# Adaptive attention and expert kernel on one core: the first three slots of a software pipeline written out one by one

## The chip, the cores and the metric

The kernel runs on one core of a Trainium2 chip. The metric is the device time of one execution in microseconds (us), the median of the runs shown. The engines of the core are TensorE (PE in the profile, with PEld for its weight loads), VectorE (DVE), ScalarE (ACT), GpSimd (POOL) and SyncE (SP). SP and ACT also issue DMA transfers from queues of their own (SPq, ACTq), and POOL issues the gathers.

## The reference

The input x has 64 samples of 64 rows and 1024 columns. With one adapter (A, B) out of 64 and one 64x64 mixing matrix for each sample:

```python
z  = (x @ B[i].T) @ A[i].T                     # rank 16
f  = rfft(z); corr = irfft(f * conj(f))        # autocorrelation of each row, length 1024
w, delay = top_k(corr, 6); w = softmax(w)
x  = x + sum_k w[k] * roll(z, -delay[k])
u  = einsum('bct,bcd->bdt', x, W[cond])        # a 64x64 matrix for each sample
p  = top_k(softmax(u @ W_router.T), 2), normalised
x  = x + u @ W_base.T + b_base + 2 * sum_e p[e] * (u @ A_stack[e].T) @ B_stack[e].T
```

All is float32 to the outside.

## The kernel before

A tile is two samples, 128 rows of x, so there are 32 tiles. Adapters are prepared in groups of eight samples, one group for four tiles. For a group the kernel loads A (eight transfers of 64 KB), sets the samples side by side (`a_beside`, ACT), transposes (`a_transposed`, PE, then `a_out`, ACT), folds it about its symmetry axes (`folds`, POOL), transposes the folds (`fold_transposed`, `fold_out`) and multiplies them by cosines and sines (`a_spectrum`, 18 matmuls). Both A and its spectrum are split in a high and a low part (`g_hi`, `g_lo`), since products of float32 accuracy are made of three matmuls (`three`). For each tile three rectangles of `g_hi` and `g_lo` are copied by DMA into one stack of 96 partitions, `adapter` (`load_adapter`), so that one matmul for 128 columns does the three products at once.

The main loop has slots s = 0 to 34. Slot s does the attention part of tile s, and, `LAG` = 3 slots later, the feed-forward part of tile t = s - 3. The steps of tile s in a slot are: transposes of x (`x_transposed`, `x_out`), x times B (`b_times_x`, `bx_masked`, `bx_repeated`), `stack_high` and `stack_low`, `spectrum` (8 matmuls), its square (ACT), `powers` (POOL, six instructions), `adapter_out` for the values y, which go to DRAM, `eo_hi` and `eo_lo`, and `correlation` (14 matmuls of 256 columns). In the next slot DVE finds the six largest (`top_delays`, L876 to L896), POOL gathers five rolled rows of y from DRAM (`gather`, L1085), and DVE adds them with their weights (`add_y` L909, `add_rolled` L917). `mixed` (PE) then multiplies by the mixing matrices, and the feed-forward part is `project` (L556), `router`, `base` (96 matmuls of 512 columns) and `experts`.

Each engine executes its own list of instructions in the order written, and waits on semaphores. `correlation(s)` is the last thing of a slot on PE; `project(t)` the first of the next. Ahead of the slots, each engine has a prologue written by hand. The eight blocks of W_base are loaded, transposed (`w_transposed`), and split (`w_high` on ACT, `w_low` on DVE): blocks 0 to 5 before slot 0, blocks 6 and 7 in slot 0. The lists of SP and PE begin so:

```python
            load_a(0)
            load_row(0)
            sp.wait_ge(bst_side, 1)
            load_b(0, row[2])
            ...
            load_mix(0)
            load_adapter(0, 0, 0)
            for m in range(KC - 2, KC):
                load_w(sp, m)
            load_a(1)
            slots(slot)
```

ACT first issues the loads of the expert and router weights, which PE transposes before all else, L645 and L646. In slots 0 to 2 there is no feed-forward part.

## Time and profile before

| | |
|---|---|
| median of 3 runs | 867.39 us (866.89 to 869.89) |
| the profiled execution | 867.77 us, with a span of 865.8 us from first to last instruction |
| PE busy | 782.6 us, 90% of the span |
| DVE, POOL, ACT busy | 655.7, 531.1, 328.9 us |
| TensorE clock granted, mean | 0.965 of full speed |
| first `project` (start of slot 3) | 108.90 us |
| ends of the first two correlations | 62.1 and 83.9 us |

All positions are microseconds from the start of the span. "Busy" leaves out waits. An engine's list of idle times names what ended each wait.

### The profile page before, as it was taken

What the parts mean: (1) busy time and instruction counts of PE and PEld (TensorE: products, weight loads), DVE (VectorE), ACT (ScalarE), POOL (GpSimd) and SP (SyncE); (2) the same over time, 40 slices, a digit from 0 to 9 for tenths busy, and PEclk for the clock granted to TensorE, in tenths of its full rate; (3) what the DMA queues carried; (4) which work ended last, traced back from release to release, by engine and by line L of the source; (5) the groups of instructions that cost most, each with busy time, mean ns of one, the idle gap of its engine ahead of it and who ended that gap; (6) DMA issues with size and microseconds to landing.
All of it is one profiled execution on the core that took longest, in us unless ns stands there. A gap on an engine that the chain in (4) does not pass through costs nothing.

```text
span 865.8 us, 14359 instructions
## 1 busy us (share of the span) xinstructions
PE 782.6 (90%) x4808; PEld 650.5 (75%) x4808; DVE 655.7 (76%) x1362; ACT 328.9 (38%) x616; POOL 531.1 (61%) x464
## 2 busy tenths in 40 slices
PE   5655699899998999899998999899998999999897
PEld 4544588778877888778786888778886888878686
DVE  1335588987888787987878888888878888888852
ACT  4453334334443434334443335334443333333211
POOL 0326576846686666856486676856696676666621
PEclk9756699999999999999999999999999999999999
DMA  8477678776877688776877698786878687786621
GB/s 269 139 226 222 193 252 256 243 242 196 268 239 243 211 259 256 241 238 196 252 243 238 210 279 240 225 231 219 259 242 240 216 251 246 240 242 197 192 76 48
DMA packets 65804, 194.26 MB, mean 224 GB/s; under 512 B 13596, under 2 KB 23228, under 8 KB 62532
## 3 DMA queue, kind: packets, MB, share of 16 engines
q0 software_dynamic: 23040, 83.90, 32.4%
q1 hardware_dynamic: 30932, 70.80, 28.4%
q10 hardware_dynamic: 11760, 38.66, 11.6%
q8 instruction: 38, 0.62, 0.3%
q14 instruction: 34, 0.28, 0.1%
HBM read 117.82 MB, written 50.33 MB: 194 GB/s over the span
## 4 chain that ended last, share of the span: by engine, by line
PE 51%; POOL 18%; DVE 13%; issue 6%; ACT 5%; DMA 4%; SPq 1%; ACTq 1%; POOLq 0%; DVEq 0%
PE o_ps L437 25%; POOL turn L1108 5%; PE h_ps L556 5%; PE x_ps L461 4%; PE c_ps L437 4%; POOL rolled L1085 4%; PE x_ps L545 3%; POOL row L1071 3%; DVE row L917 3%; POOL eo L1111 3%; POOL eo L1112 3%; DMA y_d<-y 2%; PE t_ps L514 2%; PE t_ps L491 2%; ACT eo_hi L791 2%
## 5 line engine op out<-in xcount | busy, mean ns | idle before, releaser
L1085 POOL DMA_INDIRECT rolled<-y_d,off x160 | 209.1, 1307 | 202.5 <-DVE mirror L885 97.5
L917 DVE SCALAR_TENSOR_TENSOR row<-rolled,weight,row 128x1024 f32<-128x1024 f32 x160 | 221.2, 1383 | 12.5 <-DMA rolled<-y_d,off 6.6
L437 PE MATMUL o_ps<-wt_hi,x_hi 128*128 128x512 f32 x512 | 219.9, 429 | 0.0
L437 PE MATMUL o_ps<-wt_hi,x_lo 128*128 128x512 f32 x512 | 203.3, 397 | 0.0
L437 PE MATMUL o_ps<-wt_lo,x_hi 128*128 128x512 f32 x512 | 203.0, 396 | 0.0
L437 PEld LDWEIGHTS o_ps<-wt_hi,x_hi 128*128 128x128 f32 x512 | 97.5, 190 | 22.0 <-issue 4.6
L437 PEld LDWEIGHTS o_ps<-wt_hi,x_lo 128*128 128x128 f32 x512 | 96.4, 188 | 23.3
L437 PEld LDWEIGHTS o_ps<-wt_lo,x_hi 128*128 128x128 f32 x512 | 97.1, 190 | 15.5
L1071 POOL TENSOR_TENSOR row<-row,bias 128x1024 f32<-128x1024 f32 x32 | 78.0, 2437 | 17.8 <-PE x_ps L545 17.2
L731 ACT ACTIVATE turn<-t_ps 128x512 f32<-128x512 f32 x64 | 34.9, 596 | 132.4 <-PE t_ps L491 132.4
L1108 POOL TENSOR_TENSOR turn<-turn 128x256 f32<-128x256 f32 x64 | 74.3, 1180 | 2.6
L545 PEld LDWEIGHTS x_ps<-mix,row 128*128 128x128 f32 x512 | 61.6, 192 | 16.5 <-ACT r L677 12.0
L545 PE MATMUL x_ps<-mix,row 128*128 128x128 f32 x512 | 63.0, 276 | 11.0 <-ACT r L677 9.4
L556 PE MATMUL h_ps<-aw,turn 128*128 128x136 f32 x512 | 64.6, 279 | 0.0
L556 PEld LDWEIGHTS h_ps<-aw,turn 128*128 128x128 f32 x512 | 61.7, 190 | 0.1
L858 DVE TENSOR_TENSOR eo_lo<-eo,eo_hi 128x640 fp32r<-128x640 f32 x32 | 26.4, 824 | 43.8 <-ACT eo_hi L791 43.7
L942 DVE TENSOR_SCALAR rp<-rex,rinv 128x2 f32<-128x2 f32 x32 | 58.1, 1817 | 1.1
L763 ACT ACTIVATE turn<-t_ps 128x1024 f32<-128x1024 f32 x32 | 32.8, 1025 | 62.6 <-PE t_ps L514 62.6
L858 DVE TENSOR_TENSOR x_lo<-x_ps,x_hi 128x512 fp32r<-128x512 f32 x64 | 42.6, 687 | 17.5 <-ACT x_hi L804 17.5
L437 PE MATMUL c_ps<-back_hi,eo_hi 128*128 128x256 f32 x128 | 39.4, 308 | 16.0 <-DVE eo_lo L858 16.0
L1104 POOL TENSOR_TENSOR eo<-turn 1x128 f32<-1x128 f32 x32 | 14.9, 466 | 60.6 <-ACT turn L763 60.6
L802 ACT ACTIVATE turn<-x_ps 128x512 f32<-128x512 f32 x64 | 38.1, 596 | 27.9 <-PE x_ps L545 27.9
(129 smaller groups left out, 1464.8 us busy)
## 6 DMA issues: line engine op xcount, KB each, us to landing
y_d<-y ACTq DMA_DIRECT2D x64, 512.0 KB
row<-in_x SPq DMA_DIRECT2D x32, 512.0 KB, 7.4
adapter<-g_hi SPq DMA_DIRECT2D x64, 256.0 KB, 5.4
out<-row SPq DMA_DIRECT2D x32, 512.0 KB, 6.0
adapter<-g_lo SPq DMA_DIRECT2D x32, 256.0 KB, 5.7
r<-in_L_cond_A SPq DMA_DIRECT2D x64, 64.0 KB, 4.0
r<-in_L_cond_B SPq DMA_DIRECT2D x56, 64.0 KB
rolled<-in_L_ffn_W_base SPq DMA_DIRECT2D x5, 512.0 KB, 6.1
```

Source lines behind the costliest of these rows:

```text
L437: last = pe.matmul(dst, a, b, start=start and n == 0, stop=stop and n == len(todo) - 1)
L461: return pe.matmul(dst, ft[0:rows, c, :], dft_m[0:rows, at0:at0 + width], start=start, stop=stop, skip_group_check=True)
L545: last = pe.matmul(x_ps[:, c * P:(c + 1) * P], row[t % NROW][:, c * P:(c + 1) * P], mix[t % NMIX][:, :], start=True, stop=True)
L556: last = pe.matmul(h_ps[:, 0:HW], x2[:, c, :], aw[:, c, :], start=c == 0, stop=c == KC - 1)
L731: act.activation(xt[:, 4 * h:4 * h + 4, :].rearrange("p k c -> p (k c)"), t_ps[:, h * 512:(h + 1) * 512], ACT.Copy).then_inc(xt_out, 1)
L802: act.activation(x2[:, 4 * h:4 * h + 4, :].rearrange("p k r -> p (k r)"), x_ps[:, h * 512:(h + 1) * 512], ACT.Copy).then_inc(x2_f, 1)
L858: return dve.tensor_tensor(dst, src, hi.bitcast(F32), ALU.subtract)
L917: dve.scalar_tensor_tensor(rows[:, :], from_buffer[:, :], weight[:, n:n + 1], rows[:, :], ALU.mult, ALU.add).then_inc(sum_step, 1)
L942: step(dve.tensor_scalar(rp[:, :], rex[:, :], rinv[:, :], LORA_SCALE, ALU.mult, ALU.mult))
L1071: pool.tensor_tensor(rows[:, :], rows[:, :], bias[:, :], ALU.add).then_inc(biased, 1)
L1085: pool.indirect_dma_start(out=rolled[at % RB][:, :], out_offset=None, in_=y2_d[u], in_offset=bass.IndirectOffsetOnAxis(ap=off[s % 2][:, n: ...
L1108: step(pool.tensor_tensor(pw[a], pw[a], sq[:, a, 1, :, :].rearrange("p h r -> p (h r)"), ALU.add), a == 1)
```

## The change

Slots 0 to 2 are taken out of the loop, which now begins at `FILL` = 3. Their steps are written out on each engine in a new order, together with the preparation of the weights.

```diff
+            half = GS // 2
+            first = []
+            for s in range(half):
+                first.append(sample_id(s, NS - 1))
+                sample_a(s, first[s])
             load_row(0)
+            for s in range(GS):
+                sample_b(s, first[s] if s < half else sample_id(s, NS - 1), row[4])
+            load_w(sp, 0)
+            (b_stack, a_stack, w_router: 3 loads)
+            second = [sample_id(GS + s, NS - 1) for s in range(GS)]
+            sp.wait_ge(g_h, 1); sp.wait_ge(g_lo_at, 1); sp.wait_ge(f1, 3)
+            for s in range(GS):
+                sample_a(s, second[s])
+            load_w(sp, 1) ... load_w(sp, 3); load_adapter(1, 1, 0); load_row(1); load_w(sp, 4)
+            load_mix(0); load_mix(1); load_adapter(2, 2, 0); load_row(2)
+            load_w(sp, 5); load_w(sp, 6); load_mix(2); load_adapter(3, 3, 0); load_w(sp, 7)
+            load_b(1); load_row(3); (bias); load_mix(3)
+            slots(slot, FILL)
```

ACT issues the load of the identity, then samples 4 to 7 of A, then the cosine tables. `folds(0)` and `folds(1)` run on DVE, as does the low part of A of group 0; later groups stay on POOL. Tile 0 uses `g_hi` and `g_lo` where they are, with three matmuls for each product:

```diff
+            def spectrum0():
+                for c in range(KC):
+                    cols = slice(c * P, (c + 1) * P)
+                    last = three(t_ps[:, cols], [((g_hi[0:TR, 1, cols], g_lo[0:TR, 1, cols]),
+                                                  (s_t[0:TR, :], s_low0))], True, True)
+            def adapter_out0():
+                for h in range(2):
+                    last = three(t_ps[:, cols], [((s_t[0:TR, :], s_low0),
+                                                  (g_hi[0:TR, 0, cols], g_lo[0:TR, 0, cols]))], True, True)
```

PE's list becomes:

```diff
+            a_transposed(0); x_transposed(0); b_transposed(0, row[4], o_ps); fold_transposed(0)
+            b_times_x(0, 0, 0); w_transposed(0); a_spectrum(0, False); bx_repeated(0)
+            a_spectrum(0, True); aw_transposed(); spectrum0(); w_transposed(1); adapter_out0()
+            w_transposed(2); a_transposed(1); x_transposed(1); b_times_x(1, 1, 0); bx_repeated(1)
+            correlation(0)
+            w_transposed(3); spectrum(1, 1, 0); adapter_out(1, 1); fold_transposed(1)
+            w_transposed(4); bs_transposed(); x_transposed(2); b_times_x(2, 2, 0); bx_repeated(2)
+            correlation(1)
+            w_transposed(5); spectrum(2, 2, 0); a_spectrum(1, False); adapter_out(2, 2)
+            a_spectrum(1, True); w_transposed(6); w_transposed(7); mixed(0)
+            correlation(2)
+            slots(slot, FILL)
```

A block of W is now transposed, and split, in two halves of four chunks, always through `o_ps`, and each block has a buffer of its own. On ACT, slot work of tile 1 is ordered exp(0), fold_out(1), w_high(4), y_copy(1), y_store(1), eo_high(1), x_out(2). On DVE the order around the correlations is: folds(1), top_delays(0), weights(0), add_y(0), w_low(3), add_rolled(0,0), w_low(4), eo_low(1), bx_masked(2), add_rolled(0,1), stack_low(2), top_delays(1), bs_low, add_rolled(0,2), w_low(5), add_rolled(0,3), add_rolled(0,4), spectrum_low(1), w_low(6), weights(1), add_y(1), w_low(7), add_rolled(1,0), eo_low(2), mixed_low(0), add_rolled(1,1), add_rolled(1,2). On POOL: powers(0), gather(0, first three), powers(1), gather(0, last two), gather(1, first three), powers(2), gather(1, last two), a_low(1), wait for the bias. The loop body from slot 3 on is unchanged.

## Rows read from the trace of the kernel before

**Rows 1.** The page: busy time of the engines
```profile
PE 782.6 (90%) x4808; PEld 650.5 (75%) x4808; DVE 655.7 (76%) x1362; ACT 328.9 (38%) x616; POOL 531.1 (61%) x464
```

**Rows 2.** Windows: before the first three correlations end, and the rest; last columns clock, DMA share, GB/s
```profile
0.00:62.05 62.05, 35.77 (x190) 29.84 (x191) 15.54 (x14) 29.41 (x34) 13.05 (x23) 0.78 0.70 212
62.05:83.91 21.86, 10.70 (x60) 8.74 (x59) 12.86 (x25) 6.60 (x11) 15.62 (x19) 0.63 0.73 217
83.91:108.90 24.99, 17.63 (x86) 13.46 (x85) 15.19 (x30) 9.59 (x16) 12.68 (x12) 0.71 0.68 205
108.90:865.80 756.90, 718.46 (x4480) 598.44 (x4478) 612.08 (x1293) 283.34 (x555) 489.77 (x411) 1.00 0.73 226
```

**Rows 3.** Timeline of the preparation of group 0
```profile
3.76 8.18 SPq L350 DMA_DIRECT2D r<-in_L_cond_A  x8
...
12.37 1.97 PE L443 MATMUL o_ps<-const,r 128*128 128x128 f32 x8
...
17.30 1.09 PE L443 MATMUL x_ps<-const,r 128*128 128x128 f32 x8 [1.26 <-ACT r L677]
...
18.43 2.08 ACT L677 ACTIVATE r<-x_ps 128x512 f32<-128x512 f32 x2
...
20.59 1.26 POOL L1047 TENSOR_TENSOR r<-r 128x511 f32<-128x511 f32 x1 [19.21 <-ACT r L677]
...
26.82 0.19 POOL L1061 COPY r<-r 128x2 f32<-128x2 f32 x1
```

**Rows 4.** Timeline from the spectrum of group 0 to tile 0's first product
```profile
31.32 4.45 PE L461 MATMUL x_ps<-dft_m,r 128*128 128x258 f32 x18
...
45.58 1.94 PE L514 MATMUL t_ps<-s_t,adapter 96*128 96x128 f32 x8 [2.38 <-DMA adapter<-g_hi]
```

**Rows 5.** Chain of waits, last transfer of group 1's A
```profile
53.57 3.17 DMA r<-in_L_cond_A
```

**Rows 6.** Costliest groups of DVE and ACT up to 110 us, busy us and mean ns
```profile
L917 DVE SCALAR_TENSOR_TENSOR row<-rolled,weight,row 128x1024 f32<-128x1024 f32 x8 | 10.6, 1328 | 5.1 <-DMA rolled<-y_d,off 4.7
L858 DVE TENSOR_TENSOR wt_lo<-o_ps,wt_hi 128x1024 fp32r<-128x1024 f32 x5 | 6.1, 1223 | 10.2 <-ACT wt_hi L677 10.2
L858 DVE TENSOR_TENSOR bs_lo<-o_ps,bs_hi 128x1024 fp32r<-128x1024 f32 x1 | 2.0, 2034 | 16.4 <-ACT bs_hi L677 16.4
L858 DVE TENSOR_TENSOR x_lo<-x_ps,x_hi 128x512 fp32r<-128x512 f32 x2 | 1.4, 692 | 0.3 <-ACT x_hi L804 0.3
L956 DVE TENSOR_TENSOR eo<-t_ps,const 128x128 f32<-128x128 f32 x3 | 0.8, 283 | 0.0
L786 ACT ACTIVATE t_ps<-y 128x1024 f32<-128x1024 f32 x3 | 3.1, 1028 | 2.7 <-ACT y L775 2.7
```

**Rows 7.** Windows of PE alone: busy, clock granted, DMA share
```profile
26.00:30.00 4.00, 2.93 (x14) 0.50 0.88 330
30.00:34.00 4.00, 4.00 (x23) 0.96 0.02 5
92.00:98.00 6.00, 6.00 (x18) 0.50 0.92 309
```

**Rows 8.** Timeline of slots 2 and 3 on PE and DVE
```profile
91.17 5.09 PE L461 MATMUL x_ps<-dft_m,r 128*128 128x258 f32 x10
...
97.65 3.72 PE L461 MATMUL x_ps<-dft_m,r 128*128 128x256 f32 x8
...
116.64 0.29 DVE L956 TENSOR_TENSOR eo<-t_ps,const 128x128 f32<-128x128 f32 x1 [0.50 <-PE t_ps L501]
```

**Rows 9.** Chain of waits: two correlations, base products, a stacked spectrum
```profile
80.59 2.90 PE c_ps L437 x12
107.15 1.67 PE c_ps L437 x12
113.19 2.80 PE o_ps L437 x12
...
119.78 0.84 PE t_ps L514 x8
```

More of the change, by code:

```diff
@@ L669, in _ @@
[L669 to L671 removed]
+            pe.wait_ge(w_l, 2)
+            aw_transposed()
+            spectrum0()
+            pe.wait_ge(st_out, 3)
+            w_transposed(1)
+            adapter_out0()
+            w_transposed(2)
+            a_transposed(1)
+            x_transposed(1, 0)
+            x_transposed(1, 1)
+            b_times_x(1, 1, 0)
+            bx_repeated(1)
+            pe.wait_ge(back_l, 1)
+            correlation(0)
@@ new lines, in _ @@
+            act.wait_ge(cleared, 1)
+            act.dma_start(mid_st, v["back"][:, 4 * Q:5 * Q]).then_inc(back_in, 16)
+            a_out(0)
+            a_high(0, 3, -1)
+            x_out(0, -LAG)
+            b_out(0, o_ps)
+            fold_out(0)
+            w_high(0)
+            stack_high(0)
+            act.wait_ge(back_in, 32)
+            copy(back_hi[:, 0:4, :].rearrange("p a c -> p (a c)"), back_st[:, :]).then_inc(back_h, 1)
+            copy(back_hi[:, 4, :], mid_st).then_inc(back_h, 1)
@@ L838, in _ @@
+            y_copy(0)
+            y_store(0, 0)
+            a_beside(1)
             w_high(2)
-            a_high(0, 3, -1)
-            act.wait_ge(back_in, 32)
-            copy(back_hi[:, 0:4, :].rearrange("p a c -> p (a c)"), y[:, :]).then_inc(back_h, 1)
-            copy(back_hi[:, 4, :], turn[:, 0:Q]).then_inc(back_h, 1)
-            fold_out(0)
-            b_out(0, o_ps)
+            eo_high(0)
+            x_out(1, -LAG)
+            a_out(1)
+            stack_high(1)
+            side_by_side(b_side, b_st).then_inc(bst_side, 1)
@@ L845, in _ @@
             w_high(3)
-            act.wait_ge(back_h, 2)
-            x_out(0, -LAG)
-            spectrum_high(0)
+            square(1)
+            exp(0)
+            fold_out(1)
             w_high(4)
-            stack_high(0)
-            w_high(5)
-            slots(slot)
+            y_copy(1)
+            y_store(1, 1)
+            eo_high(1)
+            x_out(2, -LAG)
+            act.wait_ge(st_ps, 2)
+            stack_high(2)
+            copy(bs_hi[:, :].rearrange("q (p j) -> q j p", j=KC),
+                 x_ps[:, :].rearrange("q (j p) -> q j p", j=KC)).then_inc(bs_h, 1)
@@ L855, in _ @@
+            w_high(5)
+            square(2)
+            exp(1)
+            a_high(1, 2, 0)
+            spectrum_high(1)
+            w_high(6)
+            w_high(7)
+            y_copy(2)
+            y_store(2, 2)
+            eo_high(2)
+            mixed_out(0)
+            slots(slot, FILL)
         @blk.vector
@@ L1023, in _ @@
-            for m in range(3):
-                w_low(m)
-            dve.wait_ge(back_h, 1)
-            low(back_lo[:, :, :].rearrange("p a c -> p (a c)"), y[:, :],
-                back_hi[:, 0:4, :].rearrange("p a c -> p (a c)")).then_inc(back_l, 1)
-            w_low(3)
-            spectrum_low(0)
-            w_low(4)
-            bx_masked(0)
-            stack_low(0)
-            w_low(5)
-            slots(slot)
+                    mixed_low(m)
+            folds(dve, 0)
+            dve.wait_ge(g_h, 1)
@@ new lines, in _ @@
+            w_low(1)
+            w_low(2)
+            eo_low(0)
+            bx_masked(1)
+            stack_low(1)
+            folds(dve, 1)
+            dve.wait_ge(ident_in, 16)
+            top_delays(0, 0)
+            weights(0)
+            add_y(0)
+            w_low(3)
+            add_rolled(0, 0)
+            w_low(4)
+            eo_low(1)
+            bx_masked(2)
+            add_rolled(0, 1)
+            stack_low(2)
+            top_delays(1, 1)
+            dve.wait_ge(bs_h, 1)
@@ new lines, in _ @@
+            low(bs_lo[:, :].rearrange("q (p j) -> q j p", j=KC), x_ps[:, :].rearrange("q (j p) -> q j p", j=KC),
+                bs_hi[:, :].rearrange("q (p j) -> q j p", j=KC)).then_inc(bs_l, 1)
+            add_rolled(0, 2)
+            w_low(5)
+            add_rolled(0, 3)
+            add_rolled(0, 4)
+            spectrum_low(1)
+            w_low(6)
+            weights(1)
+            add_y(1)
+            w_low(7)
+            add_rolled(1, 0)
+            eo_low(2)
+            mixed_low(0)
@@ L1037, in _ @@
+            add_rolled(1, 1)
+            add_rolled(1, 2)
+            slots(slot, FILL)
         @blk.gpsimd
```

423 lines of the change are left out of this document (248 added, 175 removed).

## Prediction

> **What bounds the kernel now.** I read the page first: PE is busy 90% of the span, ahead of DVE with 76% [rows 1]. Then windows cut at the ends of the first three correlations, since the change touches only what lies before slot 3. From 108.9 us on, PE is busy 718.5 of 756.9 us, 95%, at full clock: a stretch bound by PE, 23.7 us a slot, which the change leaves alone. Before it PE is busy 36 of 62, 11 of 22 and 18 of 25 us, with a mean clock of 0.78, 0.63 and 0.71 [rows 2]. These 108.9 us are filling, bound by no engine but by a chain through all of them, and only they can shrink. DMA is 0.68 to 0.73 busy in both parts [rows 2], so there is room for the same bytes in less time, though not much.
>
> Third, the timeline and the chain of waits through the fill. The reader is to see three late things. The eight A transfers take 8.2 us to issue, A is first transposed at 17.3 because work on other weights stands ahead of it, and the folds keep POOL from 20.6 to 27.0 [rows 3]. The spectrum's products are done at 35.8, yet tile 0's first product begins at 45.6, released by the DMA that copies the adapter into its stack [rows 4]. And A of group 1, transposed ahead of correlation 0, lands at 56.7 [rows 5].
>
> **The walk through the new order.** I follow the three stretches up to each correlation's end, at 62.1, 83.9 and 108.9 before [rows 2]. Ends of instructions overlap by about 0.1 us, which I let cancel against semaphore delays.
>
> *To correlation 0.* An A load costs 8.18/8 = 1.02 us of issue [rows 3]; four on each queue, from 3.8, end at 7.9. With 3.2 us to land [rows 5], A is in at 11.2. ACT's placing it side by side takes 1.05 (as other 1,024-column copies, 1.03 [rows 6]): 12.3. Eight transposes at half clock take 1.97 [rows 3]: 14.3; `a_out` 2.08 [rows 3]: 16.5. The folds on DVE: two of 511 columns at 0.69 [rows 6], four of 256 at 0.42 (between 0.28 for 128 and 0.69 for 512 [rows 6]), two tiny ones at about 0.15: 3.4 with everything, so 19.9, where POOL ended at 27.0. DVE has nothing else then, so this costs nothing. B's eight loads stand behind x of tile 0 on SP. Four cost 1.02 each; four have their ids already read, which is between nothing and 1.02, and I take 0.6 as the middle: issued by 15.3, with bounds 2 us either side that mostly vanish behind the folds, and landed about 18.5; its transposes end at 20.5, the folds' at 22.4 at the slower level. With `fold_out` (1.0) the spectrum starts at 23.5 to 24.0 and takes 4.45 [rows 4] plus 0.2 for `bx_repeated`: 28.4, where it was 35.8. The high and low parts (1.03 and 1.22 [rows 6]) end at 30.8; the transposes of the expert weights, now here, fit beside them. `spectrum0` is 24 matmuls of 128 columns. The nearest rows are the stacked product of tile 3 at full clock, 0.84/8 = 0.105, and that of tile 0 at half clock, 1.94/8 = 0.24 [rows 4, 9]. So 24 cost 2.5 to 5.8 us; I take 2.5, for a clock that has risen by then. It ends at 33.3, where the stacked product ended at 47.5. Then the square 1.0, `adapter_out0` 6 x 0.23 = 1.4 (2.80/12 [rows 9]), the copy of y 1.0, the issue of its stores and the square for corr0 2.0, group 1's A side by side 1.05, w_high(2) 1.1, eo_high 0.75, x_out(1) 1.1, bx of tile 1 0.8 and the correlation 1.9 (1.67 + 0.24) at full, 3.2 at half clock [rows 9]: 45.4 to 46.7. I take 46.2, which is 15.9 us earlier than 62.1. Powers of tile 0 (4 us from 34.4) end before eo_high starts at 41.
>
> *To correlation 1 (21.8 us before).* folds(1) wait for the last `a_out(1)` and stand on DVE before top_delays(0): they end about 2.6 us after the correlation. That is where the gain of the first folds is paid back, since POOL did group 1's under other work. Behind them: top_delays 3.8, exp and weights 0.9, add_y 1.3 [rows 6], w_low(3) 1.4, the transposes of block 4 1.1, half of w_high 0.7, y copy 1.0, stores and square 2.0, x transposes of tile 2 1.0, x_out 1.1, bx 0.9, correlation 1.9: 17.1. So 19.7 at full clock. PE is nearly idle for 6 us before block 4, so I add 0.9 for its transposes and half of 0.6 and 1.3 for those of x and the correlation: 21.7. With all at half clock and top_delays slowed by POOL as in the first of slot 1 it is 25.2. POOL's powers(1), after three gathers, end near 58.5, ahead of eo_high at 61. So nothing is won here.
>
> *To correlation 2 (25.0 before).* top_delays 3.8, bs_low 2.0 [rows 6], which now holds `x_ps` and so group 1's spectrum: 5.8. The spectrum with adapter_out(2) inside is 4.8 at full clock; at half it is 5.09 + 3.72 + 1.2 = 10.0 [rows 8]. Then high part 1.0, w_high(6) 1.1, half of w_low 0.7 [rows 6], weights and add_y 1.7, y copy 1.0, stores and square 2.0, eo_high and low 1.6, correlation 1.9 and waits of 2.0 (blocks 6 and 7 alternate in `o_ps`): 23.6 in full, 28.8 with the spectrum at half. PE waits nearly 4 us before that spectrum, so half clock is likelier; weighted three to one, and 0.4 for the rest: 27.9. Slot 2 gets 2.9 us longer.
>
> *Slot 3.* add_rolled(1,1) and (1,2), 1.33 each [rows 6], now stand behind mixed_low(0) on DVE, so top_delays(2) starts 2.6 us later in the slot, and gather (1,4), which needs (1,1), is late too. `bx_masked(3)` stood at 116.6, 7.7 us into the slot, after DVE had waited just 0.5 us for PE [rows 8]. So nearly all of a delay on DVE reaches PE's `bx_repeated(3)` and the spectrum behind it, 2 to 4 us, of which the base blocks between can hide part. I take 2.5 us, bounds 1 and 4. The bias, loaded last, lands about when POOL first needs it.
>
> The sum: 46.2 + 21.7 + 27.9 + 2.5 = 98.3 against 108.9, a gain of 10.6. The profiled execution took 867.8 (2.0 outside its span), 0.4 above the median: 857.2 us. All-full clock with the smallest terms: 45.4 + 19.7 + 23.6 + 1 = 89.7, a gain of 19.2, 848.6. Half clock in all legs but the first spectrum: 46.7 + 25.2 + 29.2 + 4 = 105.1, a gain of 3.8, 864.0.
>
> **Two rules weighed.** The eight A loads stand behind two 512 KB loads of expert weights before, and behind one of 68 KB after; with two queues issuing they save 4 x 1.02 = 4.1 us of issue [rows 3]. The Trainium skill, "DMA: Bandwidth & Descriptors", section Issuing engines are not separate DMA queues, says that all queues share the same 16 DMA engines and a second issuing engine saves only issue time. By it, if the data itself is the limit, A lands some 3 us later and the time is 860; the trace before can't show this case.
>
> **Rivals.** (a) *Full clock throughout*, 848.6 to 852. For it: after the transposes at 27 us the clock went from 0.50 to 0.96 and stayed there through the first spectrum [rows 7]. Against: gaps of 4 and 6 us on PE remain.
>
> (b) *Half clock in legs 2 and 3*, with DVE slowed: 861 to 866. For it: slots 1 and 2 before, clock 0.63 and 0.71 [rows 2].
>
> (c) *The first spectrum at half clock: slower.* In slot 2 PE was fully busy from 92 to 98 at clock 0.50 [rows 7], with spectrum products. If PE is not at full clock by 24 us, the spectrum costs 4.4 more, the expert transposes 2.5, `spectrum0` 3.3, `adapter_out0` 1.5, and the other transposes and small products up to correlation 0 about 6, each at twice its full-clock price: 17.7, in all 875. The point that decides is the clock at 24 us; should it rise at 30, only the spectrum's part is lost, 862. Against it: PE does transposes without a gap from 18.5 to 24, like those from 27 to 30 before, behind which the clock rose [rows 7].
>
> The Trainium skill, "TensorE: Matmul & The Clock Gate", Part 1, says the throttled level is the default and that activity releases it while idling brings it back. The trace agrees, save for the busy half-clock stretch; by the rule alone the gaps make (b), not (a).
>
> (d) *The gain is given back*: the loop from slot 3 runs behind POOL's gathers and powers, starts earlier but stalls until they catch up: within 0.5% of before, 864 to 868. For it: PE's 0.5 us of slack in slot 3 and two gathers out of turn. Against: 95% busy PE later [rows 2] and that these delays are at most two instructions long.
>
> **Chances.** Forecast (852 to 861) 0.52; (a) 0.16; (b) 0.16, of which 0.06 above 863.1; (c) 0.08; (d) 0.08. 0.5%, 4.3 us, is what a measurement can tell from no change. So faster 0.52 + 0.16 + 0.10 = 0.78, same 0.14, slower 0.08. The range of 850 to 865 leaves out about 0.06 of (a), 0.07 of (c) and 0.07 of (b) and (d) together: 2 in 10.
>
> **What would show it.** In the new profile: A transposed at 12.3 and folds done at 20; the clock at full by 24 and `spectrum0` done by 33 to 34; correlation ends near 46, 68 and 96; the clock of group 1's spectrum, 4.5 or 9 us; `project` first at 95.8, and bx_masked(3) about 10 us after. The forecast is wrong if leg 2 or 3 is over 5 us off, if weight loads stall PE's list (block 7 is issued behind six other transfers), or if the slots after 3 take other than 23.7 us.

## The result, and the profile after

The changed kernel takes 863.91 us (median of 16 runs, 859.34 to 866.86), beside 868.12 us (864.26 to 876.2) for the kernel before on the same chips. The ratio is 0.9939, with a 95% interval of 0.9914 to 0.9965: 0.3% to 0.9% faster, some 5 us (4.2 between the medians). The forecast was 857.2 us, a gain of 10.6. The time lies within the forecast's range, and the size of the gain is about half of the forecast one. The profiled execution after took 866.46 us, with a span of 864.6; that of before 867.77 and 865.8.

The page after answers to [rows 1]: PE and DVE a few us busier, POOL 27 us less, the folds of groups 0 and 1 among them.

```profile
PE 787.2 (91%) x4828; PEld 655.8 (76%) x4828; DVE 660.5 (76%) x1387; ACT 330.4 (38%) x624; POOL 503.7 (58%) x447
```

Windows of the changed kernel up to the ends of the correlations 0, 1 and 2, and the rest. The columns are those of [rows 2]; the third number from the end is the granted clock.

```profile
0.00:53.50 53.50, 34.22 (x188) 28.10 (x189) 12.76 (x23) 24.36 (x34) 4.41 (x14) 0.84 0.70 205
53.50:74.90 21.40, 12.77 (x84) 10.95 (x83) 13.98 (x36) 10.68 (x17) 9.84 (x11) 0.73 0.80 241
74.90:101.90 27.00, 17.80 (x84) 14.80 (x83) 20.05 (x36) 11.49 (x19) 7.33 (x10) 0.75 0.77 230
101.90:864.60 762.70, 722.46 (x4479) 601.92 (x4478) 613.71 (x1294) 283.89 (x555) 482.11 (x412) 0.99 0.73 224
```

With the ends read from the timelines, the walk of the prediction stands so (us; each leg runs from the end of one correlation's last product to that of the next; the instruction behind it begins up to 0.2 us earlier, which is where [rows 2] and the windows above are cut):

| | leg to corr. 0 | to corr. 1 | to corr. 2 | to corr. 3 | end of corr. 3 |
|---|---|---|---|---|---|
| before | 62.1 | 21.8 | 25.1 | 22.5 | 131.6 |
| forecast | 46.2 | 21.7 | 27.9 | before + 2.5 | 121.0 |
| after | 53.5 | 21.5 | 27.1 | 24.6 | 126.7 |

Three of the four legs came out within 0.8 us. The first missed by 7.3. The others gave some 1.5 of it back, and a gain of 10.6 at correlation 3 became one of 4.9.

Now the timeline of the changed kernel, from A to tile 0's first products, which answers to [rows 3] and [rows 4]:

```profile
3.45 3.56 ACTq L944 DMA_DIRECT2D r<-in_L_cond_A  x4
3.56 3.77 SPq L364 DMA_DIRECT2D r<-in_L_cond_A  x4
...
7.90 6.38 SPq L367 DMA_DIRECT2D row<-in_L_cond_B  x8
...
9.78 1.06 ACT L795 ACTIVATE r<-r 128x1024 f32<-128x1024 f32 x1
...
10.98 1.94 PE L507 MATMUL x_ps<-const,r 128*128 128x128 f32 x8 [10.98 <-ACT r L795]
...
17.76 0.16 DVE L335 COPY r<-r 128x2 f32<-128x2 f32 x1
...
19.35 1.97 PE L507 MATMUL o_ps<-const,row 128*128 128x128 f32 x8 [3.25 <-DMA row<-in_L_cond_B]
...
29.97 1.22 DVE L1012 TENSOR_TENSOR g_lo<-x_ps,g_hi 128x1024 fp32r<-128x1024 f32 x1 [2.27 <-ACT g_hi L795]
...
31.82 0.30 PE L501 MATMUL t_ps<-s_t,g_hi 32*128 32x128 f32 x1
...
36.19 0.41 PE L501 MATMUL t_ps<-s_t,g_lo 32*128 32x128 f32 x1
```

A is in 1.4 us earlier than forecast (placed from 9.8 on, against 11.2), and the folds end at 17.9 (19.9). B lands 0.8 us late (19.3, against 18.5), and behind its transposes the walk holds to within half a us: `g_lo` is done at 31.2, against 30.8. Then the matmuls of `spectrum0` grow from 0.27 to 0.41 us in the midst of it, at 32.4. The windows of PE alone (busy, granted clock, DMA share, GB/s) show why:

```profile
28.00:32.00 4.00, 4.00 (x22) 1.00 0.80 306
32.00:36.00 4.00, 4.00 (x23) 0.56 0.95 199
36.00:40.00 4.00, 4.00 (x15) 0.50 0.74 272
```

PE stands still nowhere here (it has been busy without a pause since 19.4), and its clock falls to half. The rest of the first leg on PE and ACT:

```profile
36.53 1.97 PE L670 MATMUL o_ps<-const,rolled 128*128 128x128 f32 x8
38.43 0.79 PE L501 MATMUL t_ps<-g_hi,s_t 32*128 32x512 f32 x1
...
41.45 1.02 ACT L873 ACTIVATE y<-t_ps 128x1024 f32<-128x1024 f32 x1 [2.32 <-PE t_ps L501]
42.50 1.73 ACTq L879 DMA_DIRECT2D y_d<-y  x2
44.28 1.03 ACT L880 ACTIVATE t_ps<-y 128x1024 f32<-128x1024 f32 x1 [1.80 <-issue]
...
45.33 1.04 ACT L795 ACTIVATE r<-r 128x1024 f32<-128x1024 f32 x1
46.42 1.97 PE L507 MATMUL x_ps<-const,r 128*128 128x128 f32 x8 [3.17 <-ACT r L795]
...
51.63 0.36 PE L501 MATMUL c_ps<-back_hi,eo_hi 128*128 128x256 f32 x1
...
53.25 0.28 PE L620 MATMUL c_ps<-back_hi,eo_lo 128*128 128x256 f32 x1
```

PE is idle for 3.2 us ahead of 46.42, released by ACT's `a_beside(1)`, which stands behind both stores of y and the square. Group 1's A transposes wait for it, and in PE's list x of tile 1 waits behind them, and correlation 0 behind x.

### The profile page after: what moved, and what is told of

Same layout as the page of the kernel before. It is cut to its first block, busy times and chain, and to the rows that moved or that the text cites. A ratio compares the mean times of both kernels' runs of the same rounds, so it can differ in the third digit from the quotient of the medians.

```text
span 864.6 us, 14435 instructions
## 1 busy us (share of the span) xinstructions
PE 787.2 (91%) x4828; PEld 655.8 (76%) x4828; DVE 660.5 (76%) x1387; ACT 330.4 (38%) x624; POOL 503.7 (58%) x447
## 3 DMA queue, kind: packets, MB, share of 16 engines
q10 hardware_dynamic: 10560, 35.75, 10.6%
## 4 chain that ended last, share of the span: by engine, by line
PE 49%; POOL 18%; DVE 12%; issue 5%; ACT 4%; DMA 3%; ACTq 0%; POOLq 0%; DVEq 0%
PE o_ps L501 25%; POOL turn L1285 5%; PE h_ps L639 5%; PE x_ps L525 4%; PE c_ps L501 4%; PE x_ps L628 3%; POOL rolled L1262 3%; POOL eo L1288 3%; POOL eo L1289 3%; POOL row L1246 2%; DMA rolled<-y_d,off 2%; DVE row L1071 2%; PE t_ps L597 2%; PE t_ps L574 2%; ACT eo_hi L887 2%
## 5 line engine op out<-in xcount | busy, mean ns | idle before, releaser
L1262 POOL DMA_INDIRECT rolled<-y_d,off x160 | 197.8, 1236 | 240.6 <-DVE mirror L1039 108.2
L501 PEld LDWEIGHTS o_ps<-wt_hi,x_hi 128*128 128x128 f32 x512 | 98.1, 192 | 22.2 <-issue 5.0
L501 PEld LDWEIGHTS o_ps<-wt_hi,x_lo 128*128 128x128 f32 x512 | 96.9, 189 | 23.5
L1285 POOL TENSOR_TENSOR turn<-turn 128x256 f32<-128x256 f32 x64 | 72.1, 1146 | 2.6
L1012 DVE TENSOR_TENSOR x_lo<-x_ps,x_hi 128x512 fp32r<-128x512 f32 x64 | 42.8, 686 | 19.4 <-ACT x_hi L895 19.2
L1096 DVE TENSOR_SCALAR rp<-rex,rinv 128x2 f32<-128x2 f32 x32 | 54.3, 1697 | 1.1
L1063 DVE SCALAR_TENSOR_TENSOR row<-y,weight,row 128x1024 f32<-128x1024 f32 x32 | 50.3, 1571 | 1.1
```

Source lines behind the costliest of these rows:

```text
L501: last = pe.matmul(dst, a, b, start=start and n == 0, stop=stop and n == len(todo) - 1)
L1012: return dve.tensor_tensor(dst, src, hi.bitcast(F32), ALU.subtract)
L1063: dve.scalar_tensor_tensor(rows[:, :], y[:, :], weight[:, 5:6], rows[:, :], ALU.mult, ALU.add).then_inc(sum_step, 1)
L1096: step(dve.tensor_scalar(rp[:, :], rex[:, :], rinv[:, :], LORA_SCALE, ALU.mult, ALU.mult))
L1262: pool.indirect_dma_start(out=rolled[at % RB][:, :], out_offset=None, in_=y2_d[u], in_offset=bass.IndirectOffsetOnAxis(ap=off[s % 2][:, n: ...
L1285: step(pool.tensor_tensor(pw[a], pw[a], sq[:, a, 1, :, :].rearrange("p h r -> p (h r)"), ALU.add), a == 1)
```

## Experiments

Every kernel below is the changed kernel with the edit shown. Ratios are to the kernel before, run beside each (11 to 35 runs of it, medians 866.65 to 868.33); they are taken from all the runs and not from the two medians. The ends of the correlations come from one profiled execution of each. Kernels that are alike up to correlation 0 (after, the order, folds of group 1, both bias waits, the late dummies) have it at 52.9 to 54.2, so differences of a us there say nothing. By the intervals, only five differ from after: slower are the first 17 dummies, the correlations first and the two with bias waits on all slots, faster is the last. What is said of the others rests on positions in their traces.

| kernel | us | ratio, 95% | ends of correlations 0 to 3 |
|---|---|---|---|
| after | 863.91 | 0.9939 (0.9914 to 0.9965) | 53.5, 75.0, 102.1, 126.7 |
| one queue for A | 867.57 | 0.9988 (0.9961 to 1.0015) | 56.0, 78.9, 106.0, 130.6 |
| folds(0) on POOL | 862.89 | 0.9943 (0.9917 to 0.997) | 54.4, 75.7, 103.7, 128.5 |
| folds(1) on POOL | 863.14 | 0.9951 (0.9928 to 0.9973) | 53.4, 74.9, 102.6, 127.3 |
| tile 0 by the stack | 865.18 | 0.9963 (0.9944 to 0.9982) | 57.1, 77.6, 105.5, 130.1 |
| correlations first | 869.07 | 1.0011 (0.9988 to 1.0034) | 52.0, 77.0, 109.3, 134.0 |
| `a_beside(1)` early | 863.18 | 0.9944 (0.9921 to 0.9966) | 50.8, 72.4, 100.8, 125.6 |
| expert transposes doubled | 866.14 | 0.9968 (0.994 to 0.9996) | 55.5, 76.4, 103.7, 128.3 |
| 128 rows for tile 0 | 862.24 | 0.9929 (0.9904 to 0.9953) | 55.2, 74.5, 102.9, 127.6 |
| 60 dummies | 865.34 | 0.9981 (0.9951 to 1.0012) | 59.8, 79.7, 104.2, 130.2 |
| first 17 dummies | 869.86 | 1.0024 (1.0004 to 1.0044) | 60.0, 82.5, 109.4, 134.0 |
| 60 dummies and order | 865.61 | 0.995 (0.9924 to 0.9976) | 59.0, 80.8, 104.4, 129.2 |
| later 43 dummies | 862.26 | 0.9933 (0.9906 to 0.9959) | 54.1, 74.6, 98.2, 125.5 |
| order on DVE | 867.18 | 0.9967 (0.9941 to 0.9993) | 52.9, 74.4, 101.6, 128.5 |
| bias waits | 867.91 | 1.0001 (0.9986 to 1.0015) | 53.4, 74.9, 102.1, 126.7 |
| order and bias waits | 866.96 | 0.9992 (0.9978 to 1.0006) | 54.2, 76.3, 103.4, 126.8 |
| early and later 43 | 858.40 | 0.9891 (0.9864 to 0.9919) | 51.2, 72.2, 95.7, 121.8 |
| all of these | 857.43 | 0.9887 (0.9866 to 0.9907) | 51.1, 72.2, 95.8, 120.5 |

### What the first leg gained, and from what

**One queue for A.** All eight loads go back to SP.

```diff
-            for s in range(half):
+            for s in range(GS):
                 first.append(sample_id(s, NS - 1))
                 sample_a(s, first[s])
...
-                sample_b(s, first[s] if s < half else sample_id(s, NS - 1), row[4])
+                sample_b(s, first[s], row[4])
...
-            for s in range(GS // 2, GS):
...
-                act.dma_start(a_dst[:, s, :], a_src[bass.ds(n, 1)].rearrange("o p f -> (o p) f")).then_inc(a_in, 16)
```

> The changed kernel with all eight A loads of group 0 issued by SP, none by ACT. Theory: the second queue saves only the issue time of four loads, about 3.7 us; A is placed side by side at about 13.5 instead of 9.8 and, as everything up to spectrum0 follows from it, correlation 0 is 3 to 4 us later and the time 3 to 4 us longer. Rival (x, B or the cosine tables arrive last, so A's landing is not what counts): correlation 0 moves by less than 1 us.

From its timeline:

```profile
3.70 8.18 SPq L364 DMA_DIRECT2D r<-in_L_cond_A  x8
...
12.45 3.62 SPq L367 DMA_DIRECT2D row<-in_L_cond_B  x8
13.28 1.06 ACT L795 ACTIVATE r<-r 128x1024 f32<-128x1024 f32 x1 [7.95 <-DMA r<-in_L_cond_A]
```

A is placed 3.5 us later (13.28 against 9.78), and correlation 0 ends 2.5 later, the others 3.9: the second queue is worth that. It issues the same bytes in 3.8 us instead of 8.2. The rest hides behind B, whose loads, with all ids already read, take 3.62 us here and 6.38 after. The Trainium skill, "DMA: Bandwidth & Descriptors", section Issuing engines are not separate DMA queues, says that a second engine saves the issue time only; the trace agrees, but that time is the larger part of these transfers.

**folds(0) on POOL.**

```diff
-            folds(dve, 0)
...
+            folds(pool, 0)
             powers(0)
```

> The changed kernel with folds(0) alone back on POOL. Theory: POOL takes 6.4 us where VectorE takes 2.9, so the folds are done 3.5 us later, at 21.4, but B's transposes on PE end at 21.3 in any case, so the fold transposes start under 0.5 us later: correlation 0 and the time move by less than 1 us. Rival (the folds are on the path in full): 3 to 3.5 us later and longer.

The folds end at 21.5 instead of 17.9, and B's transposes at 22.2: they hide behind B, as expected. Correlation 0 moves by 0.9 us, within the scatter, and the ratio doesn't move. The engine of the folds is no part of the gain.

**Tile 0 by the stack.** Tile 0 takes its adapter from the stack again, as in slot 0 of before, by three copies that stand ahead of those of tile 1.

```diff
+            load_adapter(0, 0, 0)
             load_adapter(1, 1, 0)
...
-            spectrum0()
+            spectrum(0, 0, 0)
...
-            adapter_out0()
+            adapter_out(0, 0)
```

> The changed kernel with tile 0 through the adapter stack as before: three more copies by DMA, 8 and 2 matmuls instead of 24 and 6. Theory: the copies issued at 31.2 land at about 37, so the spectrum ends at 39 instead of 36.5, but adapter_out is then 1.7 us cheaper at half clock: correlation 0 is 0.5 to 2 us later, not the 11 us by which tile 0's first product moved ahead in the change. Rival (in-place use is what the gain to correlation 0 is made of): 5 us or more later.

```profile
39.26 1.97 PE L598 MATMUL t_ps<-s_t,adapter 96*128 96x128 f32 x8 [5.04 <-DMA adapter<-g_hi]
```

The copy releases the first product 7.4 us later (39.26 against 31.82), but one stacked pass takes 1.97 us in place of 4.7 (31.82 to 36.5). The balance is 3.6 us at correlation 0 and 3.4 at correlation 3, between the two expectations: that is what using the adapter in place is worth by the traces, while the intervals of the two times overlap.

**Correlations first.** The x transposes of tiles 1 and 2 go behind correlations 0 and 1.

```diff
             a_transposed(1)
+            correlation(0)
             x_transposed(1, 0)
...
             bx_repeated(1)
-            correlation(0)
...
+            correlation(1)
             x_transposed(2, 0)
...
             bx_repeated(2)
-            correlation(1)
```

> The changed kernel with correlations 0 and 1 ahead of the x transposes of tiles 1 and 2 instead of behind. Theory: correlation 0 ends at 51.5 to 52.5 and correlation 1's end comes 1 to 2 us earlier too, but bx_masked of the next tile, which VectorE does ahead of top_delays, comes later by the length of the correlation, so the top_delays start no earlier and slots get no shorter: the time is the same or 1 to 3 us longer. Rival (x ahead of the correlations is what costs the missing time to correlation 0): 2 us or more shorter.

Correlation 0 ends 1.6 us earlier, 0.9 ahead of the earliest of the like kernels, and the next legs take 25.0 and 32.4 us, for 21.5 and 27.1. At correlation 3, 7.3 us are lost, more than either theory had, and with them the gain. Of the parts tried alone, x ahead of the correlations is worth most. It costs 1 to 2 us in leg 1 and pays back in legs 2 and 3, where the next tile's products would otherwise be late.

**`a_beside(1)` early.** ACT sets group 1's A side by side before it squares tile 0's spectrum.

```diff
+            a_beside(1)
             square(0)
...
             y_store(0, 0)
-            a_beside(1)
```

> The changed kernel with one move: on ScalarE group 1's a_beside stands ahead of square(0), where ScalarE waits 3.4 us, instead of behind tile 0's y_store. Theory: it, then a_transposed(1), stood in line before correlation 0; now a_transposed(1) follows w_transposed(2) at 43, x_transposed(1) follows y_store at about 44.5, and correlation 0 ends 2 to 4 us earlier, 50 to 51.5. The time is 2 to 4 us shorter. Rival (correlation 0 waits for powers and eo_high alone): it moves by under 1 us.

```profile
34.85 1.07 ACT L795 ACTIVATE r<-r 128x1024 f32<-128x1024 f32 x1
...
43.41 1.91 PE L507 MATMUL x_ps<-const,r 128*128 128x128 f32 x8
```

A of group 1 had landed by 35 us. Its transposes start 3.0 us earlier (43.41 against 46.42) without a wait, and correlation 0 ends at 50.8, 2.7 earlier. The two later kernels with this move have it at 51.2 and 51.1, so this is no scatter: the wait on PE in the timeline of the first leg was on the path. At correlation 3 1.1 us are left (leg 3 took 28.4).

### The clock

**Expert transposes doubled.** Is it that the small products ahead of `spectrum0` leave the array too little to do? Each full transpose is made twice, with the same result.

```diff
                     pe.transpose(dst[:, 0:P], a_st[:, k * P:(k + 1) * P], ident)
+                    pe.transpose(dst[:, 0:P], a_st[:, k * P:(k + 1) * P], ident)
```

> The changed kernel with each of the eight full 128x128 transposes in aw_transposed done twice into the same place (8 more, about 1 us of PE, mostly beside the splitting of the spectrum). Theory A (the clock falls at 32.4 us, with PE busy without a gap, because the stretch is made of small matmuls: 8-row transposes, then 32-row products): with denser full-size work the clock stays full longer, spectrum0 ends by 35 instead of 36.5 and correlation 0 ends 3 to 6 us earlier, near 48 to 50. Rival B (the clock falls for another reason, or its moment is chance): correlation 0 ends at 53.5 to 55, the added work is lost or hidden, the time is unchanged or 1 us longer.

The matmuls of `spectrum0`, which began at 34.2, went from 0.27 to 0.41 us at 34.8. In kernels that are like the changed one up to there the fall came at 32.4 (after), 33.7 (folds of group 1), 35.3 (order), 35.7 (`a_beside(1)` early) and 35.8 (bias waits), so it was not put off. Correlation 0 ended 1.9 later. The theory fell.

**128 rows for tile 0.** Is it the 32 rows? Both operands of tile 0's products get 128 rows, those of s being zero from row 32 on (the edit of `spectrum0`; `adapter_out0` has the same).

```diff
-    ((g_hi[0:TR, 1, cols], g_lo[0:TR, 1, cols]), (s_t[0:TR, :], s_low0))
+    ((g_hi[:, 1, cols], g_lo[:, 1, cols]), (s0[:, 0, :], s0[:, 1, :]))
```

> The changed kernel with spectrum0 and adapter_out0 as products over 128 rows instead of 32: the small operand lies in a cleared 128-row buffer, so the results and the number of matmuls and columns are the same. Theory A (matmuls that use few rows let the granted clock fall although PE has no gap): the clock stays full through spectrum0, which ends by 34.5 us instead of 36.5, adapter_out0 takes 1.6 us instead of 2.9, and correlation 0 ends near 49 to 50. Rival B (what the rows hold plays no part): the clock falls at 32 to 35 us as in the other runs and correlation 0 ends at 52.5 to 55.

The clock fell at 34.5 us and correlation 0 ended at 55.2. That theory fell too. The time of 862.24 us is not shown to differ from that of after.

**60 dummies.** PE's gaps are filled with products of 512 columns whose result nobody reads: 7 between the chunks of `spectrum0` (not shown), 10 before `a_transposed(1)`, and then 18, 11 and 14 as shown.

```diff
+            def busy(dst, n):
+                for _ in range(n):
+                    pe.matmul(dst, back_hi[:, 0, 0:P], back_hi[:, 0:2, :].rearrange("p a c -> p (a c)"),
+                              start=True, stop=True)
...
+            busy(h_ps[:, :], 10)
             a_transposed(1)
...
+            busy(h_ps[:, :], 18)
             w_transposed(4)
...
+            busy(h_ps[:, :], 11)
             a_spectrum(1, False)
...
+            busy(h_ps[:, :], 14)
             correlation(2)
```

> The changed kernel with 60 added matmuls of 512 columns whose results are overwritten unread: one after each of seven chunks of spectrum0, and 10, 18, 11 and 14 in the gaps of PE before a_transposed(1), w_transposed(4), a_spectrum(1) and correlation(2). Each costs 0.23 us at full and 0.43 at half clock, about 14 us of PE in all, nearly all inside idle time if the clock holds. Theory (the missing 7 us to correlation 0, and 4 more to slot 3, are half clock): clock full from 22 us on but for short falls, correlation ends at 48 to 50, 68 to 71 and 91 to 96 instead of 53.5, 74.8 and 101.9, and the time is 4 to 9 us shorter. Rival (PE follows the other engines anyway, and the added work is in its way): correlation ends no earlier than now, time 0 to 5 us longer.

Windows of PE alone:

```profile
32.00:36.00 4.00, 4.00 (x21) 1.00 0.33 68
36.00:44.00 8.00, 8.00 (x23) 0.50 0.69 204
44.00:52.00 8.00, 8.00 (x27) 0.50 0.60 149
52.00:56.00 4.00, 4.00 (x24) 0.86 0.42 167
```

For 17 us PE is busy without a gap at half clock, some twelve of the dummies among its products. So the fall at 32.4 to 36.5 us, which the changed kernel and all 17 variants have, is not that of an idle array. Two more readings narrow it down. In all 18 the first stretch at full clock runs for 10.2 us, whether it begins at 22.2 (after) or at 26.2 (tile 0 by the stack, where PE even waits from 34.2 to 39.3). The fall keeps its distance from the rise and not from any product. And the load on DMA doesn't sort the stretches: its share is 0.80 at full clock from 28 to 32 in after, 0.74 at half clock from 36 to 40, and 0.73 at nearly full clock (0.99) from 101.9 on. Legs 2 and 3 are another matter: 19.9 and 24.5 us, for 21.5 and 27.1.

**The first 17 dummies alone.** Against the kernel with 60:

```diff
-            busy(h_ps[:, :], 18)   (and 11, and 14)
```

> Only the first 17 of the added matmuls: seven inside spectrum0, ten before a_transposed(1). Theory: full clock up to correlation 0, which ends at 48 to 50 instead of 53.5; from there the legs take 21.4 and 27.1 as now; the time is 2 to 4 us shorter. Rival (the clock falls at 32 to 35 whatever PE does): correlation 0 at 55 to 57, the time 2 us longer.

Correlation 0 at 60.0, legs 2 and 3 at 22.5 and 26.9: the early dummies cost 6.4 us and win nothing behind them. The 7 within `spectrum0` stretch it from 4.8 to 10.3 us (34.2 to 44.5), mostly at half clock; the other 10, 3.7 us in all, stand where PE had waited 3.2.

**The later 43 alone.**

> The changed kernel with only the later 43 added matmuls (18, 11 and 14, in PE's gaps before w_transposed(4), a_spectrum(1) and correlation(2)). Theory (half clock in the last two stretches costs what the run with all 60 showed, 1.4 and 2.6 us): correlation 0 ends at 53 to 54, the next two follow after 20 and 24.5 us (21.4 and 27.1 now), project takes 1.9 us, and the time is 3 to 5 us shorter unless slot 3 meets the slow add_y. Rival: no gain, as the added work delays PE.

Windows of this kernel between the ends of correlations 0, 1 and 2:

```profile
53.90:74.40 20.50, 15.44 (x102) 12.77 (x101) 13.72 (x36) 10.53 (x16) 9.85 (x11) 0.87 0.81 253
74.40:98.10 23.70, 20.60 (x109) 17.43 (x109) 19.93 (x35) 11.56 (x19) 9.32 (x10) 0.90 0.81 257
```

The granted clock is 0.87 and 0.90 where it was 0.73 and 0.75, and the legs take 20.5 and 23.6 us: 4.5 won, with 43 more products on PE. The five kernels with these dummies need 44.1 to 45.4 us for the two legs, those without them that keep the order of PE's list 47.7 to 50.1. Half clock in legs 2 and 3 is shown to cost this. In this execution slot 3 lost most of it again (27.4): PE waited 1.9 us for `bx_masked(3)`, of which the next part treats, and from 109.9 to 116.7 its clock was at half. With the same wait at full clock, the kernel of `a_beside(1)` early and the later 43 has 26.1.

**60 dummies with the order of slot 3 mended.**

> All 60 added matmuls and add_rolled(1,1) ahead of eo_low(2). Theory: as the first, with slot 3 at 22.8 to 24 us instead of 24.8, unless add_y of slot 3 meets the bias addition (4.1 us instead of 1.3), when it is 26 to 27. The time is that of the first, or 1 us less.

Legs 21.8 and 23.6, slot 3 24.7, where the 60 dummies alone had 26.0. The medians don't differ (865.61 and 865.34); only the traces tell the two apart.

### Leg 2 and slot 3

**folds(1) on POOL.**

```diff
-            folds(dve, 1)
...
             powers(0)
+            folds(pool, 1)
```

> The changed kernel with folds(1) alone back on POOL, behind powers(0). Theory: VectorE starts top_delays(0) right after correlation 0, 2.4 us earlier than now, but runs beside POOL's folds, which slow its small instructions as before (6.0 instead of 3.7 us); the two cancel, correlation 1 follows correlation 0 after 20 to 22 us (21.35 now) and the time is the same within 1 us. Rival (moving the folds to VectorE is what costs here): 19 us and a time 2 us shorter.

Leg 2 is 21.4 us (21.5 after), and the ratio is the same: it makes no difference to leg 2 which of the two engines folds group 1.

**Order on DVE.** `add_rolled(1,1)` goes ahead of `eo_low(2)`.

```diff
             add_rolled(1, 0)
+            add_rolled(1, 1)
             eo_low(2)
             mixed_low(0)
-            add_rolled(1, 1)
             add_rolled(1, 2)
```

> The changed kernel with one edit: on VectorE add_rolled(1,1) stands before eo_low(2) instead of behind mixed_low(0). Theory: the 2.2 us lost in slot 3 (correlation 2 to correlation 3 takes 24.8 us against 22.6 before) come from the two additions that stand ahead of top_delays(2) and from gather (1,4), which waits for add_rolled(1,1). Expected: top_delays(2) begins within 1.5 us of correlation 2's end, correlation 3 follows after 22.6 to 23.5 us, and the time falls by 1 to 2 us. Rival (half clock at the start of slot 3 makes it long): 24 us or more, as now, with project at about 3.1 us instead of 1.9.

First slot 3 as it is after, DVE and two rows of POOL:

```profile
100.36 2.67 DVE L1071 SCALAR_TENSOR_TENSOR row<-rolled,weight,row 128x1024 f32<-128x1024 f32 x2
102.94 0.69 DVE L1030 MAX8 val<-c_ps 128x8 f32<-128x512 f32 x1
...
103.84 2.39 POOL L1240 TENSOR_TENSOR g_lo<-r,g_hi 128x1024 fp32r<-128x1024 f32 x1
104.47 1.80 DVE L1034 TENSOR_SCALAR in_even<-idx 128x3 f32<-128x3 uint32 x1
...
111.28 0.28 DVE L1112 TENSOR_TENSOR eo<-t_ps,const 128x128 f32<-128x128 f32 x1
...
111.94 1.28 DVE L1063 SCALAR_TENSOR_TENSOR row<-y,weight,row 128x1024 f32<-128x1024 f32 x1
...
113.78 2.71 DVE L1096 TENSOR_SCALAR rp<-rex,rinv 128x2 f32<-128x2 f32 x1
...
114.06 2.39 POOL L1246 TENSOR_TENSOR row<-row,bias 128x1024 f32<-128x1024 f32 x1
```

The two late additions end 0.9 us behind correlation 2, and `bx_masked(3)` stands at 111.28, 9.4 us behind the start of `project`, where it was 7.7 before [rows 8]. The slot is 2.1 longer. Part of it is a meeting of two engines: `in_even`, an instruction of three columns in `top_delays`, takes 1.80 us instead of 0.17 and ends with POOL's `a_low(1)`, of 2.39. With the new order DVE is through `top_delays` 4.6 us behind correlation 2 instead of 6.1, yet the slot takes 26.9 us:

```profile
110.85 4.05 DVE L1063 SCALAR_TENSOR_TENSOR row<-y,weight,row 128x1024 f32<-128x1024 f32 x1
111.42 2.39 POOL L1246 TENSOR_TENSOR row<-row,bias 128x1024 f32<-128x1024 f32 x1
114.93 0.29 DVE L1012 TENSOR_TENSOR s_t<-t_ps,s_t 32x128 fp32r<-32x128 f32 x1
```

`add_y` takes 4.05 us in place of 1.28, and ends 1.1 us behind POOL's bias addition, which began after it; `stack_low`, for which PE's spectrum waits, is next on DVE. PE waits 2.0 us there. The expectation was missed, since the earlier start on DVE brought this meeting about.

**Bias waits.** In every slot POOL holds the bias addition until `stack_low` is done.

```diff
                 pool.wait_ge(x2_mm, 2 * t + 2)
+                if t + LAG < NT:
+                    pool.wait_ge(s_lo, t + LAG + 1)
                 pool.tensor_tensor(rows[:, :], rows[:, :], bias...)
```

> The changed kernel where POOL's bias addition of each slot also waits until VectorE has done stack_low of that slot. Theory: the runs so far show slots of 24.3 to 28.1 us instead of 22.6 to 23.5 exactly where add_y, which stands ahead of stack_low, takes 4.1 us instead of 1.3 because POOL's addition began beside it. With the wait add_y never takes over 1.4 us, no slot from 4 on exceeds its usual length, the time falls by 1 to 4 us and its spread shrinks. Rival (the long slots come from the gathers' transfers): they stay.

No `add_y` took over 1.5 us, and slots that are alike (every fourth) agree within 0.1 us, at 23.0 and 24.1. But their usual lengths in after are 22.6 and 23.5. About half a us in every second slot is 7 to 8 us, more than the meetings that it prevents had cost in the profiled execution of after (6.1: 24.3, 26.3 and 25.0 for 23.4, 23.5 and 22.6), and the kernel is back at the time of before.

**Order and bias waits.**

> The changed kernel with both edits: add_rolled(1,1) ahead of eo_low(2), and the bias addition waiting for stack_low. Theory: slot 3 was 27.0 us in the run with the order alone only because add_y met the bias addition; without that meeting the order shortens slot 3 from 24.8 to 23 to 23.8 us. The time is 1 us below that of the wait alone. Rival (half clock in project makes slot 3 long): 24.5 us or more.

```profile
101.81 2.93 DVE L1071 SCALAR_TENSOR_TENSOR row<-rolled,weight,row 128x1024 f32<-128x1024 f32 x1
...
106.18 0.17 DVE L1034 TENSOR_SCALAR in_even<-idx 128x3 f32<-128x3 uint32 x1
```

Slot 3 is 23.4 us where both after and the bias waits alone have 24.6: with the meeting of `add_y` out of the way, the order of the two additions is worth 1.2 us, about one of them (1.28). The meeting with `a_low(1)` is still there: it now falls on the one addition that is left ahead of `top_delays(2)`, 2.93 us, and `in_even` is back at 0.17. The rival of half clock in `project` needs a look, since `project` took 2.9 us at half clock in after and 1.8 at full clock here. It is out: folds(0) on POOL, 128 rows and `a_beside(1)` early had 1.8 as well, with slots of 24.6 to 24.8.

### Together

**`a_beside(1)` early and the later 43 dummies.**

> The later 43 added matmuls and a_beside(1) early. Theory: the two gains add, correlation ends at 50 to 51.5, 70.5 and 95 against 53.5, 74.8 and 101.9, and the time is 6 to 8 us shorter than the changed kernel, the shortest so far. Rival: the second takes the first's idle time and they do not add: 3 to 4 us.

858.40 us. Legs 51.2, 21.0 and 23.5: the two gains add up, 6.4 us at correlation 2 where the parts had 1.3 and 3.9.

**All: with the order, and the bias addition of tile 0 alone waiting.**

```diff
+                if t == 0:
+                    pool.wait_ge(s_lo, LAG + 1)
```

> The 43 later added matmuls, a_beside(1) early, add_rolled(1,1) ahead of eo_low(2), and the bias addition of tile 0 alone (slot 3) waiting for stack_low(3). Theory: slot 3 is 22.8 to 23.6 us (26.1 without the last two), later slots as in the kernel without waits, correlation ends near 51, 72, 95.5 and 119; the time is 1 to 3 us below the version without them, 856 to 858. Rival (slot 3 is long for a reason other than the order and the meeting with the bias addition): 24.5 us or more.

857.43 us, ratio 0.9887 (0.9866 to 0.9907): the fastest, 9.2 us below before, run beside it. Slot 3 took 24.7 us, not the 22.8 to 23.6 expected, though `add_y` took 1.28 in it. DVE is late: it starts `top_delays(2)` 2.5 us behind correlation 2, where it was 0.8 in after, since the correlation came earlier and the one addition ahead took 2.91 us, ending 1.1 us behind `a_low(1)`. Its ratio and that of the kernel before it overlap, so what the order adds is not shown in the time.

## Why the prediction was half right

**Which part is bound, and by what: right.** The slots from 4 on have the lengths of before but for single ones (below), and the gain lies in the fill. The sums of the forecast are right to 0.15 us.

**A, folds, B, the spectrum of group 0: right, on the safe side.** An A load took 0.9 us of issue, not 1.02, and A was in at least 1.4 us before its time; B came 0.8 late. Putting the folds on DVE was right as a cost of nothing, because B ends later than either engine's folds.

**"24 cost 2.5 to 5.8 us; I take 2.5, for a clock that has risen by then": the step that failed.** The clock had risen, by 24 us as forecast. It then fell to half at 32.4, with PE busy without a pause. No step of the walk and no rival had it fall inside the first leg. What it and the rest cost, from 30.8 on, against the forecast (whose fifth row has the 0.8 by which it went from its sum of 45.4 to 46.2):

| piece | forecast | after | lost |
|---|---|---|---|
| start of `spectrum0` | 30.8 | 31.8 | 1.0 |
| `spectrum0` | 2.5 | 4.7 | 2.2 |
| square, wait behind `w_transposed(1)`, `adapter_out0` | 2.4 | 4.9 | 2.5 |
| copy of y; stores and square | 3.0 | 3.9 | 0.9 |
| `a_beside(1)` to the correlation's start | 5.6 | 6.3 | 0.7 |
| correlation | 1.9 | 1.9 | 0 |

That makes 7.3 us. By the rows, half clock accounts for about 2 in `spectrum0` and 1.5 of the third row (2.9 for 1.4), and most of what is left of that row is `w_transposed(1)`, 1.97 us where such transposes took 1.09 at full clock. No run kept the clock up here, so these prices are read from rows and not from an experiment. The issue of the two stores took 1.73 where 1.0 was counted. The other flaw is one of method: the walk ran down ACT's list and set its pieces end to end, and did not follow PE's, where `w_transposed(1)` stands in front of `adapter_out0`, and x of tile 1 behind A's transposes, which wait for an instruction that ACT has behind the stores. Moving that instruction gave 2.7 us.

**Leg 2, 21.7: right (21.5).** The folds of group 1 end 2.3 us behind correlation 0, forecast 2.6. That the gain of the first folds is paid back there is not so: with them on POOL the leg is as long. **Leg 3, 27.9: right (27.1).** The answer lies in the rows of group 1's spectrum, beside 5.09 and 3.72 before [rows 8]:

```profile
80.60 5.25 PE L525 MATMUL x_ps<-dft_m,r 128*128 128x258 f32 x10 [2.93 <-DVE bs_lo L1012]
...
86.50 2.18 PE L525 MATMUL x_ps<-dft_m,r 128*128 128x256 f32 x8
...
101.90 3.12 PE L639 MATMUL h_ps<-aw,turn 128*128 128x136 f32 x16
```

Its first part runs at half clock behind a wait of 2.9 us on `bs_low`; the second half, forecast at half too, mostly ran at full. The later dummies show that the low clock costs 4 us in these two legs. **Slot 3, +2.5: right in size (+2.1), in part by luck.** The forecast had `top_delays(2)` start 2.6 us later in the slot; it starts 0.8 later, and `in_even` beside `a_low(1)`, which the forecast didn't have, adds 1.6.

**The rivals.** (a) Full clock throughout did not come. (b) Half clock in legs 2 and 3 names the right clock, but these legs cost what the forecast had given them; the time of (b), 861 to 866, came about by the first leg. (c) has the nearest mechanism, half clock in the first leg, but as a clock that has not risen by 24 us; it rose, and fell again at 32.4. Its price for `adapter_out0`, 1.5, is what was measured. The rule weighed ahead of the rivals, the data as the limit and A some 3 us later, did not come: A was in at 9.8. (d) Given back: slots 4 to 31 have the lengths of before, so no gathers out of turn. The profiled execution did lose 3.8 us behind correlation 3 (4.9 won there, 1.1 at the end), by three slots in which `add_y` was long:

```profile
232.62 4.16 DVE L1063 SCALAR_TENSOR_TENSOR row<-y,weight,row 128x1024 f32<-128x1024 f32 x1
233.28 2.42 POOL L1246 TENSOR_TENSOR row<-row,bias 128x1024 f32<-128x1024 f32 x1
...
282.87 1.34 DVE L1063 SCALAR_TENSOR_TENSOR row<-y,weight,row 128x1024 f32<-128x1024 f32 x1
283.90 2.51 POOL L1246 TENSOR_TENSOR row<-row,bias 128x1024 f32<-128x1024 f32 x1
```

The slots of these three took 24.3, 26.3 and 25.0 us where the same slots of before took 23.4, 23.5 and 22.6. Before had one such slot, 24.4 us, in which `weight` took 3.04 us instead of 0.23 beside the same addition. Whether the meeting happens changes from kernel to kernel and run to run, and it may make a good part of the runs' spread: with the bias waits, which keep `add_y` out of it, the spans of 12 runs have a standard deviation of 1.3 us, those of 16 runs of the changed kernel 2.1.

## What to carry to other kernels

Walk a new order down every engine's list, and begin each step at the later of its data and its place in line: what was missed here was in a second engine's list, and cost 2.7 us. In a filling phase, price every TensorE step at both clock levels until a trace shows which it has, and fill its waits with work, real or idle, only where a run shows that the clock answers: 43 dummy products won 4 us in two legs, and 17 cost 6 in the first. When an instruction of one engine moves, look at what the other engine of the pair VectorE and GpSimd does at its new place. Read transfers by their issue as well as their bytes, and let a second queue take half of many small ones.
